# Ten bias additions on GpSimd moved from the aggregation into the first stage of a graph layer with a ternary feed-forward

## Chip, cores and metric

The kernel runs on one core of a Trainium2 chip. The metric is the time on the device in microseconds (us); the kernel before takes 337.06 us, the median of three runs from 336.26 to 338.64. All times of rows count from the start of the profiled span.

## What is computed

One graph layer over 1250 nodes of 512 features and 20000 edges sorted by destination, then a gated feed-forward with ternary weights. Cut to what matters:

```python
def gnn(x, src, dst, W_self, W_neigh, b):          # x: layer-normed nodes
    msg_sum = segment_sum(x[src], dst, 1250)
    neigh = msg_sum / maximum(deg, 1.0)[:, None]
    h = x @ W_self + neigh @ W_neigh + b
    h = where(h >= 0, h, 0.01 * h)
    return h / maximum(sqrt(sum(h * h, axis=1, keepdims=True)), 1e-12)

def quantize(w, group):                            # groups of 128 along a row
    scale = mean(abs(wg), axis=-1, keepdims=True) + 1e-5
    return clip(round(wg / scale), -1, 1) * scale

x = x + gnn(layernorm(x), src, dst, W_self, W_neigh, b)
g, u = ln(x) @ quantize(w_gate).T, ln(x) @ quantize(w_up).T
x = x + (silu(g) * u) @ quantize(w_down).T
```

The change touches only the place where `+ b` is computed.

## The kernel before

The 1250 nodes are ten tiles of 125 rows. Semaphores and the order of the code alone say what runs when: each engine's block is written out by hand, and an engine works strictly in that order. Three stages matter.

**First stage, 80 slots, eight to a tile (to about 107 us).** PE multiplies each layer-normed tile `xnT` with both weight halves in `w_sb` (L1374): slots 0 to 3 of a tile give `y` (neighbour part), slots 4 to 7 give the self part in bank 6, which ACT copies into `z[:, t, :]` (L847, semaphore `z_out`) in slot 2 of the next tile. ACT also writes the high part of `y` (L844); DVE computes the low part `y_lo` (L1122) from PSUM. Between the products PE builds the matrix of edge counts `a_t`, two chunks of 128 edges a slot (L1326, 157 chunks). For each chunk DVE makes a one-hot matrix `hot_dst` with a `tensor_scalar` over 16-bit numbers (L1138), and for each eight chunks `hot_src` with a `tensor_tensor` (L1129). Seven slots of `hot_dst` let DVE run ahead of PE. ACT and DVE move finished blocks from PSUM into `a_t` (L864, L1095). Layer norm of the next tiles (bn at L1025, xn at L1018) is DVE's too.

In the same slots 23 loads of feed-forward weights are made ternary, four blocks of 128 x 128 (jobs) a load: ACT takes magnitudes and their sums (L813, semaphore `abs_done`), GpSimd makes a load's thresholds in one small `tensor_scalar` (`scales_of(l)`, L693, `thr`), and DVE compares and multiplies, one `scalar_tensor_tensor` a job (L1039, "the ternary", reading `mag` and `raw` in SBUF). There are two magnitude buffers, so ACT's load l waits for the ternaries of load l - 2. For loads 0 to 3 GpSimd also runs a few checks (`check_windows`, L702 to L723).

**Between the stages (about 107 to 113 us)** four more loads are quantized (`mag_mid`, loads 23 to 26, `MID_LOADS` = 27). The other loads (`mag_late`) follow in the aggregation.

**Aggregation (about 108 to 158 us).** For each tile n, PE sums 10 x 2 products of `a_t` with `y` (L1418). Then DVE adds the sum to `z` (L1175, `neighbour_sum`, waits for `z_done`), takes the leaky part (L1181), and, when ACT has the norm, adds to `x_sb` (L1202, the residual), with bn_stats (L1208), and `shift` (L1217). ACT normalizes (`xn`, L877), and PE transposes that tile (L1315) in the middle of its sum four tiles on, so PE waits there if `xn` is late.

The bias stands in `bias_b`, 125 x 512 for a tile. GpSimd adds it to `z` in place (L735, `add_bias(t)`, 125 x 512 floats, both inputs in SBUF) and signals `z_done`. Before the change this comes when all thresholds up to load 26 are made and the matrix is joined: two tiles, then one after the thresholds of each aggregation step, the last five in a row. After it GpSimd scales the sums (`nscale`, L745) and has nothing to do until the feed-forward, which starts near 165 us and is bound by PE (L1481).

Of the kernel before, what the change touches and what calls it, by code (L numbers as in the profile page):

```python
# [31 lines left out]
ALU = mybir.AluOpType  # L32
# [11 lines left out]
def gnn_ffn(nc, x, src, dst, w_self, w_neigh, bias, w_gate, w_up, w_down, out):  # L44
# [3 lines left out]
    TP = 125  # L48
    NT = N // TP
# [6 lines left out]
    NB = 1 + NC // SC  # L56
# [45 lines left out]
    def place(name, shape, dt, region, offset=0):  # L102
        return nc.alloc_sbuf_tensor_at(name, shape, dt, offset=at[region] + offset)

    def small(name, shape, dt):
        width = {F32: 4, F32R: 4, I32: 4, BF16: 2, U16: 2}[dt]
        for n in shape[1:]:
            width *= n
        o = used["small"]
        used["small"] = o + -(-width // 32) * 32  # L110
        assert used["small"] <= 13184, 0
        return place(name, shape, dt, "small", o)
# [5 lines left out]
    z = place("z", [TP, NT, D], F32, "xz", GAP)  # L118
# [72 lines left out]
    bias_b = small("bias_b", [P, D], F32)  # L191
# [22 lines left out]
    with ExitStack() as ctx:  # L214
# [5 lines left out]
        def sem(name):  # L220
            return ctx.enter_context(nc.semaphore(name))
# [7 lines left out]
        bias_in = sem("bias_in")  # L229
# [15 lines left out]
        z_out = sem("z_out")  # L245
        z_done = sem("z_done")
# [8 lines left out]
        joined = sem("joined")  # L255
# [40 lines left out]
        for o, f in down_loads:  # L296
            n = min(4, NF - f)
            loads.append((w_down[o * P:(o + 1) * P, f * P:(f + n) * P], n))
            down_order += [(o, f + i) for i in range(n)]
        assert (2 * NF + 4) * P * 2 >= SBS * SB * P * 2  # L300
        job_load = [(l, i) for l, (_, n) in enumerate(loads) for i in range(n)]
        JOBS = len(job_load)
        load_end = [sum(n for _, n in loads[:l + 1]) for l in range(len(loads))]
        assert JOBS == 3 * NF * KD

# [58 lines left out]
        def down_loads_in(n):  # L364

            lo, hi = (MID_LOADS + max(0, min(NL, 2 * i)) for i in (n, n + 1))
            return range(lo, hi)
# [213 lines left out]
        def _(sp):  # L581
# [46 lines left out]
            for i, (_, f, down) in enumerate(by_dma):  # L628
                if i < TURN_SLOTS:
                    sp.wait_ge(ternary, load_end[len(loads) - RAWS + i])  # L630
                else:
                    sp.wait_ge(t_done, turn_T[by_dma[i - TURN_SLOTS]] + 1)
                for a in range(1 if down else 2):
                    for k in range(KD):
                        block = tq_d[:, k, f * P:(f + 1) * P] if down else tq_gu[:, a * NF + f, k * P:(k + 1) * P]
                        sp.dma_start(turned[:, turn_slot(i), a * D + k * P:a * D + (k + 1) * P], block,
                                     transpose=True).then_inc(t_turned[i % TURN_SLOTS], 16)
# [12 lines left out]
        def _(pool):  # L650
# [38 lines left out]
            def scales_of(l):  # L689

                js = slice(load_end[l] - loads[l][1], load_end[l])
                pool.wait_ge(abs_done, load_end[l])
                nc.gpsimd.tensor_scalar(thr[:, js], absum[:, js], 0.5 / P, 0.5 * Q_EPS, ALU.mult, ALU.add).then_inc(scales, 1)  # L693

            def check_windows(part):
# [22 lines left out]
                if part == 3:  # L718
# [3 lines left out]
                    pool.wait_ge(compared, 11)  # L722
                    nc.gpsimd.tensor_scalar(gap_ok[:], gap[:], 0.0, None, ALU.is_ge).then_inc(compared, 2)  # L723

            for l in range(MID_LOADS):
                scales_of(l)
                if l < 4:
                    check_windows(l)
            pool.wait_ge(bias_in, 16)
            pool.wait_ge(joined, NB - 1)  # L730

            def add_bias(t):

                pool.wait_ge(z_out, t + 1)
                nc.gpsimd.tensor_tensor(z[:, t, :], z[:, t, :], bias_b[0:TP, :], ALU.add).then_inc(z_done, 1)  # L735

            for t in range(2):
                add_bias(t)
            for n in range(NT):
                for l in down_loads_in(n):  # L740
                    scales_of(l)
                if n + 2 < NT:
                    add_bias(n + 2)

            nc.gpsimd.tensor_scalar(nscale[:], absum[:], 1.0 / P, Q_EPS, ALU.mult, ALU.add).then_inc(nscales, 1)  # L745

# [760 lines left out]
```

## Time and profile before

| | us |
|---|---|
| median of three runs | 337.06 |
| lowest, highest | 336.26, 338.64 |
| the profiled execution | 337.36 |
| its span | 335.6 |
| PE busy in the span | 315.7 (94%) |
| DVE busy | 305.3 (91%) |
| ACT busy | 236.9 (71%) |
| GpSimd (POOL) busy | 169.5 (51%) |

The span is the part of the profiled execution in which the program's instructions run; 1.8 us lie around it. PE's granted clock is 0.997 of full speed over the span. PE's matmuls are pipelined, and a matmul's end is modelled, so neighbouring rows overlap; the start of a matmul is the surer number. The same goes for instructions of DVE and ACT that stand close behind each other: they overlap by some tens of nanoseconds.

### The profile page before, as it was taken

The page shows a single profiled execution, that of the slowest core. Times are in us where ns is not written, and L with a number is a line of the kernel's source. Part 1 is how long each engine was busy: PE and PEld are TensorE (multiplying, and loading weights), DVE is VectorE, ACT ScalarE, POOL GpSimd, SP SyncE. Part 2 cuts the span into 40 slices and gives each one's busy share as a digit, 9 for nine tenths or more (in the row PEclk, how much of TensorE's full clock was granted, in tenths as well). Part 3 has the DMA queues.
Part 4 walks back from the last instruction along what each step waited for, and adds up shares of the span by engine and source line. Part 5 has one row for each costly group of instructions (what it writes and reads, how often), then busy time and mean ns, then how long its engine had stood idle before and what let it go on. Part 6 is the DMA issues. An engine that isn't in the chain of part 4 may idle for free.

```text
span 335.6 us, 5723 instructions
## 1 busy us (share of the span) xinstructions
PE 315.7 (94%) x1521; PEld 237.5 (71%) x1521; DVE 305.3 (91%) x782; ACT 236.9 (71%) x636; POOL 169.5 (51%) x235
## 2 busy tenths in 40 slices
PE   7989999999999999789989999999999999999991
PEld 3434454444554787577858898998989988899981
DVE  3599999998996899997999999999999999999993
ACT  2178988689885666354897677867868688676760
POOL 6015100010100445600016686989889897899992
PEclk9999999999999999999999999999999999999998
DMA  7992322223330321100001111111110100000305
GB/s 216 288 225 69 94 57 71 65 63 94 98 87 27 103 82 48 27 14 0 1 17 25 24 28 26 27 25 28 25 25 21 22 2 1 2 1 1 114 11 183
DMA packets 23610, 19.62 MB, mean 58 GB/s; under 512 B 15230, under 2 KB 16084, under 8 KB 23576
## 3 DMA queue, kind: packets, MB, share of 16 engines
q1 hardware_dynamic: 23498, 19.16, 21.3%
q8 instruction: 13, 0.21, 0.3%
q14 instruction: 21, 0.17, 0.2%
q10 hardware_dynamic: 78, 0.08, 0.1%
HBM read 13.73 MB, written 2.56 MB: 49 GB/s over the span
## 4 chain that ended last, share of the span: by engine, by line
PE 58%; DVE 27%; issue 4%; ACT 3%; DMA 3%; POOL 2%; SPq 1%; DVEq 0%; ACTq 0%; POOLq 0%
PE bank L1481 43%; PE bank L1374 7%; DVE hot_dst L1138 5%; DVE tq_gu L1039 4%; DVE tq_d L1039 4%; PE bank L1418 4%; DMA x_sb<-in_x 3%; PE bank L1326 2%; DVE hot_src L1129 2%; DVE bn L1025 1%; DVE z L1175 1%; DVE z L1181 1%; DVE x_sb L1202 1%; PE bank L1315 1%; DVE bn L1208 1%
## 5 line engine op out<-in xcount | busy, mean ns | idle before, releaser
L1481 PE MATMUL bank<-x_hi,t_gu 128*128 128x376 f32 (+1 forms) x264 | 94.5, 358 | 1.6 <-DVE g_acc L1270 0.7
L1481 PE MATMUL bank<-x_lo,t_gu 128*128 128x376 f32 (+1 forms) x264 | 92.8, 351 | 0.0
L1374 PE MATMUL bank<-w_sb,xnT 128*125 128x512 f32 x160 | 82.9, 606 | 1.7 <-DMA w_sb<-in_L_gnn_W_neigh 1.3
L1270 DVE SCALAR_TENSOR_TENSOR g_acc<-bank,nscale,g_acc 128x376 f32<-128x376 f32 (+1 forms) x99 | 63.8, 644 | 3.7 <-PE bank L1481 3.3
L1270 DVE SCALAR_TENSOR_TENSOR u_acc<-bank,nscale,u_acc 128x376 f32<-128x376 f32 (+1 forms) x99 | 63.6, 643 | 0.0
L754 POOL TENSOR_TENSOR acc<-acc,d_one 128x376 f32<-128x376 f32 (+1 forms) x58 | 63.3, 1094 | 0.0
L764 POOL TENSOR_TENSOR hh<-sg,u_acc 128x376 f32<-128x376 f32 (+1 forms) x32 | 35.1, 1096 | 50.6 <-ACT sg L974 50.6
L693 POOL TENSOR_SCALAR thr<-absum 128x4 f32<-128x4 f32 (+1 forms) x34 | 9.7, 285 | 99.8 <-ACT mag_early L813 75.5
L1481 PEld LDWEIGHTS bank<-x_hi,t_gu 128*128 128x128 f32 x264 | 49.6, 188 | 7.9 <-DVE g_acc L1270 1.8
L1481 PEld LDWEIGHTS bank<-x_lo,t_gu 128*128 128x128 f32 x264 | 49.6, 188 | 3.3
L1326 PEld LDWEIGHTS bank<-hot_dst,hot_src 128*126 128x126 bf16 x157 | 20.6, 135 | 41.4 <-DVE hot_dst L1138 26.3
L1481 PE MATMUL bank<-h_hi,t_d 128*128 128x376 f32 (+1 forms) x132 | 47.6, 361 | 0.2
L1481 PE MATMUL bank<-h_lo,t_d 128*128 128x376 f32 (+1 forms) x132 | 46.6, 353 | 0.0
L1418 PE MATMUL bank<-y_hi,a_t 125*125 125x512 f32 x100 | 40.2, 402 | 0.8 <-DVE a_t L1095 0.8
L1270 DVE SCALAR_TENSOR_TENSOR acc<-bank,nscale,acc 128x376 f32<-128x376 f32 (+1 forms) x62 | 39.3, 643 | 0.6 <-POOL acc L754 0.6
L1418 PE MATMUL bank<-y_lo,a_t 125*125 125x512 f32 x100 | 39.4, 394 | 0.0
L773 POOL TENSOR_TENSOR h_lo<-hh,h_hi 128x376 fp32r<-128x376 f32 (+1 forms) x32 | 35.0, 1094 | 4.9 <-ACT h_hi L921 4.9
L911 ACT ACTIVATE d_one<-bank,nscale 128x376 f32<-128x376 f32 (+1 forms) x58 | 34.8, 604 | 1.7 <-PE bank L1481 1.7
L1138 DVE TENSOR_SCALAR hot_dst<-iota_w,key 128x140 bf16<-128x140 uint16 (+4 forms) x150 | 34.4, 270 | 0.9 <-PE bank L1326 0.8
L813 ACT ACTIVATE mag_early<-raw 128x128 f32<-128x128 f32 x92 | 27.5, 304 | 7.7 <-DVE tq_gu L1039 6.5
L911 ACT ACTIVATE g_acc<-bank,nscale 128x376 f32<-128x376 f32 (+1 forms) x33 | 20.1, 608 | 17.3 <-PE bank L1481 16.5
L1039 DVE SCALAR_TENSOR_TENSOR tq_gu<-mag_early,thr,raw 128x128 bf16<-128x128 f32 x88 | 28.8, 354 | 2.8 <-POOL thr L693 2.7
(143 smaller groups left out, 550.5 us busy)
## 6 DMA issues: line engine op xcount, KB each, us to landing
raw<-in_L_ffn_w_gate SPq DMA_DIRECT2D x11, 256.0 KB, 2.7
raw<-in_L_ffn_w_up SPq DMA_DIRECT2D x11, 256.0 KB, 2.6
out_x<-x_sb SPq DMA_DIRECT2D x10, 224.0 KB
raw<-in_L_ffn_w_down SPq DMA_DIRECT2D x8, 256.0 KB, 2.7
turned<-tq_gu SPq DMA_TRANSPOSE x80, 2.4
w_sb<-in_L_gnn_W_neigh SPq DMA_DIRECT2D x1, 1024.0 KB, 7.2
w_sb<-in_L_gnn_W_self SPq DMA_DIRECT2D x1, 1024.0 KB, 8.4
x_sb<-in_x SPq DMA_DIRECT2D x2, 448.0 KB
```

The source lines that it names most:

```text
L754: nc.gpsimd.tensor_tensor(to, to, d_one[:, o, slot, 0:width(u)], ALU.add).then_inc(d_added, 1)
L764: nc.gpsimd.tensor_tensor(hh[:, u % 2, 0:w], sg[:, u % 2, 0:w], u_acc[:, u % 2, 0:w], ALU.mult).then_inc(h_done, 1)
L773: nc.gpsimd.tensor_tensor(h_lo[:, u % h_slots, 0:w], hh[:, u % 2, 0:w], h_hi[:, u % h_slots, 0:w].bitcast(F32), ALU.subtract).then_inc(hlo ...
L813: nc.scalar.activation(mag_of(j), raw_of(j), ACT.Abs, accum_out=absum[:, j:j + 1]).then_inc(abs_done, 1)
L911: nc.scalar.activation(to, bank_of(u, what)[:, 0:width(u)], ACT.Copy, scale=nscale[:, j:j + 1]).then_inc(act_took, 1)
L1039: nc.vector.scalar_tensor_tensor(out=tq_of(j), in0=mag_of(j), scalar=thr[:, j:j + 1], in1=raw_of(j), op0=ALU.is_gt, op1=ALU.mult).then_inc ...
L1138: nc.vector.tensor_scalar(to, numbers, key[:, c:c + 1], None, ALU.is_equal).then_inc(hot_made, 1)
L1270: nc.vector.scalar_tensor_tensor(out=to, in0=bank_of(u, what)[:, 0:w], scalar=nscale[:, j:j + 1], in1=to, op0=ALU.mult, op1=ALU.add).then_ ...
L1326: nc.tensor.matmul(bank[k % 3][0:TQ, 0:NT * WIN].rearrange("p (s d) -> p s d", d=WIN)[:, :, lo:hi], hot_src[:, c // SB % SBS, c % SB, 0:TQ ...
L1374: last = nc.tensor.matmul(to[0:TP, :], xnT[:, t, k * TP:(k + 1) * TP], w_sb[:, k, half * D:(half + 1) * D], start=k == 0, stop=k == KD - 1)
L1418: last = nc.tensor.matmul(bank[4 + n % 2][0:TP, :], a_t[0:TP, s, n * TP:(n + 1) * TP], y[:, s, :], start=s == 0 and y is y_hi, stop=s == N ...
L1481: last = nc.tensor.matmul(bank_of(u, what)[:, 0:width(u)], w, parts[h], start=h == 0, stop=h == 1)
```

## The change

The ten additions leave their place behind the thresholds of load 26. They now stand in the loop over loads 0 to 26 itself: behind the threshold of load `BIAS_AT[t]` comes the addition for tile t, which still waits for ACT's copy of that tile (`z_out`). The first waits for the load of the bias. The wait for the joined matrix is gone. The instructions themselves are the same; no other engine's code is touched.

```diff
+            BIAS_AT = [4, 5, 7, 10, 12, 15, 17, 20, 22, 23]
             for l in range(MID_LOADS):
                 scales_of(l)
                 if l < 4:
                     check_windows(l)
-            pool.wait_ge(bias_in, 16)
-            pool.wait_ge(joined, NB - 1)
-
-            def add_bias(t):
-
-                pool.wait_ge(z_out, t + 1)
-                nc.gpsimd.tensor_tensor(z[:, t, :], z[:, t, :], bias_b[0:TP, :], ALU.add).then_inc(z_done, 1)
-
-            for t in range(2):
-                add_bias(t)
+                if l in BIAS_AT:
+                    t = BIAS_AT.index(l)
+                    if t == 0:
+                        pool.wait_ge(bias_in, 16)
+                    pool.wait_ge(z_out, t + 1)
+                    nc.gpsimd.tensor_tensor(z[:, t, :], z[:, t, :], bias_b[0:TP, :], ALU.add).then_inc(z_done, 1)
             for n in range(NT):
                 for l in down_loads_in(n):
                     scales_of(l)
-                if n + 2 < NT:
-                    add_bias(n + 2)
```

On GpSimd (POOL), in the first stage, these rows stand behind the last window check (`gap_ok`) in the kernel before. `thr` rows are thresholds of a load each, `z` rows are additions; the first 19 thresholds belong to the first stage, the next four to loads 23 to 26, the rest to the aggregation.

```order
L723 TENSOR_SCALAR gap_ok<-gap 128x31
L693 TENSOR_SCALAR thr<-absum 128x4 x19
L693 TENSOR_SCALAR thr<-absum 128x3
L693 TENSOR_SCALAR thr<-absum 128x4 x2
L693 TENSOR_SCALAR thr<-absum 128x3
L735 TENSOR_TENSOR z<-z,bias_b 125x512 x2
L693 TENSOR_SCALAR thr<-absum 128x4 x2
L735 TENSOR_TENSOR z<-z,bias_b 125x512
L693 TENSOR_SCALAR thr<-absum 128x4
L693 TENSOR_SCALAR thr<-absum 128x3
```

In the changed kernel, from the same `gap_ok` row on:

```order
L723 TENSOR_SCALAR gap_ok<-gap 128x31
L693 TENSOR_SCALAR thr<-absum 128x4
L735 TENSOR_TENSOR z<-z,bias_b 125x512
L693 TENSOR_SCALAR thr<-absum 128x4
L735 TENSOR_TENSOR z<-z,bias_b 125x512
L693 TENSOR_SCALAR thr<-absum 128x4 x2
L735 TENSOR_TENSOR z<-z,bias_b 125x512
L693 TENSOR_SCALAR thr<-absum 128x4 x3
L735 TENSOR_TENSOR z<-z,bias_b 125x512
L693 TENSOR_SCALAR thr<-absum 128x4 x2
L735 TENSOR_TENSOR z<-z,bias_b 125x512
```

The run of 19 thresholds (loads 4 to 22) is cut up: additions of tiles 0 to 4 stand behind the thresholds of loads 4, 5, 7, 10 and 12. Further on, those of tiles 8 and 9 stand around the threshold of load 23, the 128x3 row, and no addition stands in the aggregation.

```order
L693 TENSOR_SCALAR thr<-absum 128x4 x2
L735 TENSOR_TENSOR z<-z,bias_b 125x512
L693 TENSOR_SCALAR thr<-absum 128x3
L735 TENSOR_TENSOR z<-z,bias_b 125x512
L693 TENSOR_SCALAR thr<-absum 128x4 x2
L693 TENSOR_SCALAR thr<-absum 128x3
L693 TENSOR_SCALAR thr<-absum 128x4 x3
L693 TENSOR_SCALAR thr<-absum 128x3
L693 TENSOR_SCALAR thr<-absum 128x4 x2
```

Here the additions of tiles 8 and 9 are the two `z` rows, and everything behind them is a threshold.

## Rows read from the trace of the kernel before

**Rows 1.** Busy time of each engine in stretches; their columns stand in the first line.

```profile
core 0: us, PE busy (x) PEld busy (x) DVE busy (x) ACT busy (x) POOL busy (x), PEclk, DMA share, GB/s
35.00:60.00 25.00, 24.66 (x103) 12.91 (x103) 23.83 (x103) 22.05 (x78) 1.94 (x7) 1.00 0.23 66
...
96.00:107.00 11.00, 11.00 (x43) 5.49 (x42) 8.41 (x37) 6.62 (x17) 0.19 (x1) 1.00 0.20 59
130.00:145.00 15.00, 11.74 (x56) 9.09 (x57) 14.62 (x36) 6.08 (x20) 7.68 (x7) 1.00 0.12 25
145.00:160.00 15.00, 15.00 (x79) 12.00 (x77) 12.62 (x32) 7.45 (x19) 0.00 (x0) 1.00 0.02 4
```

**Rows 2.** The chain of waits by line: 36 to 41 us, 41 to 84, 84 to 107.

```profile
by line: issue 27.3%; ACT mag_early L813 17.3%; ACT a_t L864 11.7%; ACT xnT L850 11.6%; PE bank L1315 8.6%; PE bank L1374 8.6%; DVE tq_gu L1039 5.0%; PE bank L1326 4.4%; POOL thr L693 4.0%; ACT y_hi L844 1.4%; ACT hot_src L796 0.9%; ACTq L8
by line: DVE hot_dst L1138 26.6%; DVE tq_gu L1039 24.3%; DVE hot_src L1129 9.8%; issue 8.4%; ACT mag_early L813 5.9%; DVE bn L1025 5.7%; DVE y_lo L1122 5.5%; DVE xn L1018 4.8%; DVE a_t L1095 2.7%; ACT a_t L864 2.2%; POOL thr L693 0.9%; DVE 
by line: PE bank L1374 77.1%; PE bank L1326 17.6%; PE bank L1315 3.7%; PE bank L552 3.2%; issue 0.2%
```

**Rows 3.** Waits of PE, 107 to 145 us: total, times, longest, in us.

```profile
PE bank L1315 <- ACT xn L877: 3.7, 3, 1.9
```

**Rows 4.** GpSimd's additions in order of time: start, us, engine, line, operation, count.

```profile
113.11 2.59 POOL L735 TENSOR_TENSOR z<-z,bias_b 125x512 f32<-125x512 f32 x2
...
122.28 1.67 POOL L735 TENSOR_TENSOR z<-z,bias_b 125x512 f32<-125x512 f32 x1
...
131.79 7.18 POOL L735 TENSOR_TENSOR z<-z,bias_b 125x512 f32<-125x512 f32 x5
```

**Rows 5.** DVE in the aggregation: three instructions, then groups (busy us, mean ns, idle before).

```profile
113.07 1.48 DVE L1039 SCALAR_TENSOR_TENSOR tq_d<-mag_mid,thr,raw 128x128 bf16<-128x128 f32 x1
...
131.72 0.75 DVE L1175 SCALAR_TENSOR_TENSOR z<-bank,rdeg,z 125x512 f32<-125x512 f32 x1
...
133.55 1.78 DVE L1202 SCALAR_TENSOR_TENSOR x_sb<-z,inv,x_sb 125x512 f32<-125x512 f32 x1
...
L1039 DVE SCALAR_TENSOR_TENSOR tq_d<-mag_late,thr,raw 128x128 bf16<-128x128 f32 x26 | 9.9, 445 | 0.0
L1202 DVE SCALAR_TENSOR_TENSOR x_sb<-z,inv,x_sb 125x512 f32<-125x512 f32 x10 | 8.5, 850 | 0.1
L1175 DVE SCALAR_TENSOR_TENSOR z<-bank,rdeg,z 125x512 f32<-125x512 f32 x10 | 7.4, 744 | 1.9 <-PE bank L1418 1.9
...
L1039 DVE SCALAR_TENSOR_TENSOR tq_d<-mag_mid,thr,raw 128x128 bf16<-128x128 f32 x14 | 6.2, 503 | 0.8 <-POOL thr L693 0.7
```

**Rows 6.** DVE's three costliest groups, 36 to 84 us.

```profile
L1138 DVE TENSOR_SCALAR hot_dst<-iota_w,key 128x140 bf16<-128x140 uint16 (+4 forms) x83 | 18.9, 268 | 0.0
L1039 DVE SCALAR_TENSOR_TENSOR tq_gu<-mag_early,thr,raw 128x128 bf16<-128x128 f32 x53 | 17.3, 348 | 1.9 <-POOL thr L693 1.9
L1129 DVE TENSOR_TENSOR hot_src<-iota,hot_src 128x1000 bf16<-128x1000 uint16 x11 | 7.5, 681 | 0.0
```

**Rows 7.** A window check of GpSimd and DVE's hot_dst beside it.

```profile
22.78 0.64 POOL L702 TENSOR_TENSOR win_lo<-rel,win_lo 128x157 f32<-128x157 f32 x1
22.95 0.52 DVE L1138 TENSOR_SCALAR hot_dst<-iota_w,key 128x140 bf16<-128x140 uint16 x1
```

**Rows 8.** Thresholds (41 to 84 us as group), copies of z, hot_dst and its use, DVE's waits.

```profile
L693 POOL TENSOR_SCALAR thr<-absum 128x4 f32<-128x4 f32 x12 | 3.8, 313 | 38.1 <-ACT mag_early L813 38.1
40.55 0.19 POOL L693 TENSOR_SCALAR thr<-absum 128x4 f32<-128x4 f32 x1 [3.83 <-ACT mag_early L813]
...
108.97 0.20 POOL L693 TENSOR_SCALAR thr<-absum 128x3 f32<-128x3 f32 x1 [11.29 <-ACT mag_mid L813]
92.94 0.58 ACT L847 ACTIVATE z<-bank 125x512 f32<-125x512 f32 x1
101.29 0.59 ACT L847 ACTIVATE z<-bank 125x512 f32<-125x512 f32 x1
102.14 0.64 DVE L1138 TENSOR_SCALAR hot_dst<-iota_w,key 128x200 bf16<-128x200 uint16 x3
102.99 0.30 PE L1326 MATMUL bank<-hot_dst,hot_src 128*126 128x140 bf16 x2
DVE tq_gu L1039 <- POOL thr L693: 2.7, 4, 0.8
```

## The prediction

> **What bounds the kernel now.** I began with the table of busy time by stretch [rows 1]. From 35 to 60 us PE and DVE are both near full, 24.66 and 23.83 of 25 us. From 96 to 107 us PE is full and DVE has 8.41 of 11. From 130 to 145, in the aggregation, PE is busy for only 11.74 of 15 us while DVE has 14.62; behind 145 PE has 15.00 of 15. For the first stage the table does not say which of the two sets the pace; the chain of waits does [rows 2]. From 36 to 41 us it passes through ACT and PE and hardly touches DVE (tq_gu 5.0% alone). From 41 to 84 us it lies on DVE: hot_dst 26.6, tq_gu 24.3, hot_src 9.8, bn 5.7, y_lo 5.5, xn 4.8%, together 76.7%. From 84 to 107 us it lies on PE alone.
>
> In the aggregation the view of waits shows what DVE's lateness costs PE: its transposes wait for ACT's xn three times, 3.7 us in total, the longest 1.9 [rows 3]. ACT makes xn from DVE's residual and shift, so DVE stands behind those waits.
>
> Now the ten additions [rows 4]: two at 113.11 us take 2.59, so 1.3 us each, and five in a row 7.18. The one at 122.28 takes 1.67, so it was itself held up by 0.4. Beside them some of DVE's instructions are long [rows 5]: a ternary at 113.07 us takes 1.48, where the mean of the first stage is 0.35 [rows 6], and ends at 114.55, where the first addition does (114.4). A residual at 133.55 takes 1.78. The sum z<-bank,rdeg,z at 131.72, whose first input lies in PSUM, runs beside an addition in 0.75, its usual time (the ten of them mean 744 ns). So an addition holds one DVE instruction that reads SBUF as ternaries do, up to its own end: 1.1 us.
>
> **What the change takes away.** All ten additions leave the stretch from 113 to 139 us. What they cost DVE there follows from the means [rows 5]: 14 ternaries of mag_mid at 503 instead of 348 ns are 2.2 us, 26 of mag_late at 445 are 2.5, ten residuals at 850 instead of some 744 (a sum of the same shape) are 1.1. Together 5.8 us, and with a shift and a leak some 6.2. PE cannot take back more than it waited, 3.7 us [rows 3], because behind 145 us it is full. As DVE gets 6 us and needs 3.7, I take all of the 3.7. The lower end is 1.5, if DVE's freed time comes too late for the first two waits.
>
> The wait for the last join goes too; GpSimd had nothing else to do there. The threshold for load 26, which stood behind two additions, comes some 2 us earlier, but DVE takes it only behind the first leak. Nothing.
>
> **What it puts in.** Each addition stands behind one threshold and in front of the next. From 41 to 84 us GpSimd is idle 38.1 us before 12 thresholds [rows 8], 3.2 us each, against 1.3 for an addition: the next threshold, and the ternaries that wait for it, are not late. Tiles 7 and 8 are not copied yet at their place: ACT writes them at 92.94 and 101.29 us [rows 8], 0.6 us each, so GpSimd waits for it and adds from 93.6 and 101.9. Nothing is due before either ends. Tile 9 stands behind the threshold at 108.97 us, where DVE waits for each threshold: I count one stalled ternary, 1.1 us, and up to 0.4 for the next threshold. That is less than the 2.2 us which tiles 0 and 1 cost there before, so it costs the end nothing and eats part of DVE's 6.
>
> For the other nine the question is what DVE does beside them. From 36 to 84 us [rows 6] hot_dst has 18.9 us, the ternaries 17.3, hot_src 7.5. Ternaries and hot_src read two tensors of SBUF. That hot_dst, with one, is held too, the window checks early in the program show [rows 7]: beside GpSimd's 0.64 us at 22.78 a hot_dst takes 0.52 us where the mean is 0.27, and both end within 0.05 us of each other. What looks free (y_lo, a_t with PSUM; bn) is 5.5 + 2.7 + 5.7 = 13.9% of the chain [rows 2], a sixth of DVE's part. So some four in five additions meet an exposed instruction at once.
>
> The Trainium skill draws the same line between instructions: GPSIMD Engine Reference, section 8 (Key points), has GpSimd contend with VectorE instructions that run in a two-port mode or have two SBUF inputs, and VectorE: DVE Perf Modes, section on the perf-mode tier table, puts a 16-bit tensor_scalar from SBUF into the fastest of these modes. It speaks against this change: by that rule hot_dst stalls with each addition, and the first stage costs more than the aggregation gives back. The 0.52 us agrees. Were only two-input instructions held, the cost would go towards the low end below.
>
> One stall: 1.1 us where the next instruction is exposed, about 0.6 where a free one comes first; 0.8 x 1.1 + 0.2 x 0.6 = 1.0 us. Tile 1 stands behind the threshold at 40.55 us [rows 8], and tiles 1 to 6 all start between there and 84 us, where the chain is on DVE: 6 x 1.0 = 6.0. DVE's four waits for thresholds (2.7 us, the longest 0.8 [rows 8]) may swallow 0.4 of it. Tile 0, near 37 us, falls where the chain is not on DVE, and DVE then waits 0.7 us for that threshold anyway: of 1.1 I leave 0.4. Tile 7 falls where the chain is on PE and DVE has a wait of 0.7 ahead: nothing. Tile 8, at 101.9: of the three hot_dst from 102.14 us (0.64 together), the first is used by PE at 102.99 [rows 8], some 0.6 to 0.9 us later, so 1.1 leaves 0.3. Sum: 6.0 - 0.4 + 0.4 + 0.3 = 6.3 us. Bounds: from below six stalls of 0.5, 3.0 us (a stall like the old average, under rival 1); from above nine of 1.13 (1.48 - 0.35), 10.2. I take 6.3, since the ternaries that were met stand at 1.0 to 1.1.
>
> **The sum.** +6.3 - 3.7 = +2.6 us. The profiled execution took 337.36 us (span 335.6), so 340.0. It lies 0.3 above the median of the three runs, 337.06; against that median the forecast is 339.7 us, 0.8% more. Everything behind 145 us is only moved.
>
> **Rivals.**
> 1. Not slower: the stalls of the first stage are cheap. The ten old additions took 6.2 us from DVE, 0.6 each, because some met bn_stats or a PSUM input. At 0.5 us for tiles 1 to 6 and nothing for the others the cost is 3.0 and the change -0.7: 336.4 us. The point from which it decides is a cost of 3.7, about 0.6 for each of the six. Against it: free instructions are a sixth of DVE's part of the chain [rows 2], fewer than in the aggregation. Chance 25%.
> 2. Nothing swallows anything: nine additions delay PE by 1.1 each, because PE and DVE take turns in being late and the first stalls use up the leads. 9.9 - 3.7 = +6.2: 343.3 us. For it: both are at 95% or more [rows 1]. Against it: DVE has 2.6 us of 11 to spare behind 96 us. Chance 10%.
> 3. The aggregation gives back only 1.5 us, since tile 9's addition now delays the quantizing at 109 us, on which DVE's first sum hangs. 6.3 - 1.5 = +4.8: 341.9 us. Against it: DVE still comes out 5 us ahead of before. Chance 10%.
>
> **How the numbers follow.** My forecast has 55%, with a range of its own from 338.3 to 341.3 us. A measurement of this kernel can tell about 1% (3.4 us) from no change, so the bounds are 333.7 and 340.4. Slower by more: a third of the forecast's share (0.19), rival 2 and most of rival 3 (0.18), together 0.37. Faster by over 1% needs nearly the whole 3.7 us and no cost at all: 0.03. The rest, 0.60, lies within 1%. The range from 335.8 to 342.8 takes in rival 1, rival 3 and the forecast and leaves out most of rival 2.
>
> **What would show it.** In the changed kernel's profile: nine additions of z before the aggregation and a tenth right behind the first mag_mid threshold; beside six to eight of them a hot_dst, hot_src or ternary of 1.2 to 1.5 us; that threshold, at 108.97 us now, some 6 us later; no long residual or leak in the aggregation, and PE's waits for xn gone. The forecast is wrong if hot_dst beside an addition keeps its 0.27 us, if that threshold moves by less than 4 us, or if PE still waits for xn by more than 1 us.

## The result, and the profile after

The changed kernel takes 339.93 us (median of 8 runs, 338.86 to 340.56) against 337.32 us before (8 runs): a ratio of 1.0082, 95% interval 1.0056 to 1.0108, so 1.9 to 3.6 us slower. The forecast was 339.7 us and 2.6 us. The sum came out; its terms did not quite, as the stages show.

The profiled execution has a span of 338.1 us. Two rows of PE's timeline in each kernel mark the stages: the first use of `hot_dst` and the first product with `a_t`. In the kernel before (columns: start, duration):

```profile
18.38 0.64 PE L1326 MATMUL bank<-hot_dst,hot_src 128*126 128x140 bf16 x3 [1.03 <-DVE hot_dst L1138]
...
108.25 0.50 PE L1418 MATMUL bank<-y_hi,a_t 125*125 125x512 f32 x1 [0.76 <-DVE a_t L1095]
...
163.63 0.42 PE L1481 MATMUL bank<-x_hi,t_gu 128*128 128x376 f32 x1
```

In the changed kernel:

```profile
16.79 0.64 PE L1321 MATMUL bank<-hot_dst,hot_src 128*126 128x140 bf16 x3
...
114.19 0.49 PE L1413 MATMUL bank<-y_hi,a_t 125*125 125x512 f32 x1 [0.76 <-DVE a_t L1090]
...
165.26 0.42 PE L1476 MATMUL bank<-x_hi,t_gu 128*128 128x376 f32 x1
```

Line numbers behind the change are 5 lower. The differences: the first stage goes from 89.9 to 97.4 us (+7.5), the aggregation from 55.4 to 51.1 (-4.3). The start is 1.6 us earlier, because the first loads of x and the edges landed earlier in this execution (DVE waits 0.2 us for x there, 1.3 in the profile before): over the twelve profiles of this study it lies between 16.8 and 19.2 us whatever the kernel. The feed-forward took 0.9 us more, of which below. So +7.5 - 4.3 = +3.2 us by stages, inside the interval of the times.

GpSimd's additions in the changed kernel (of tiles 1, 3, 4, 8 and 9, with the threshold of load 23 in front of the last), which answer to [rows 4]:

```profile
39.80 1.27 POOL L735 TENSOR_TENSOR z<-z,bias_b 125x512 f32<-125x512 f32 x1
...
60.48 1.53 POOL L735 TENSOR_TENSOR z<-z,bias_b 125x512 f32<-125x512 f32 x1
...
70.03 1.27 POOL L735 TENSOR_TENSOR z<-z,bias_b 125x512 f32<-125x512 f32 x1
...
107.39 1.26 POOL L735 TENSOR_TENSOR z<-z,bias_b 125x512 f32<-125x512 f32 x1 [4.14 <-ACT z L842]
...
114.92 0.20 POOL L693 TENSOR_SCALAR thr<-absum 128x3 f32<-128x3 f32 x1 [6.27 <-ACT mag_mid L808]
115.19 1.28 POOL L735 TENSOR_TENSOR z<-z,bias_b 125x512 f32<-125x512 f32 x1
```

And what DVE does beside tiles 1, 3, 4 and 8:

```profile
39.78 1.44 DVE L1034 SCALAR_TENSOR_TENSOR tq_gu<-mag_early,thr,raw 128x128 bf16<-128x128 f32 x1
...
60.71 1.38 DVE L1133 TENSOR_SCALAR hot_dst<-iota_w,key 128x220 bf16<-128x220 uint16 x1
...
70.06 1.29 DVE L1133 TENSOR_SCALAR hot_dst<-iota_w,key 128x140 bf16<-128x140 uint16 x1
...
107.35 1.36 DVE L1133 TENSOR_SCALAR hot_dst<-iota_w,key 128x140 bf16<-128x140 uint16 x1
```

Each of the nine additions in the first stage, and tile 9's too, met such an instruction at once: five ternaries and five `hot_dst`, 1.29 to 1.46 us where they have 0.35 and 0.27 alone. `hot_dst`, with one input, is held as firmly as the ternary. The `hot_dst` end 0.05 to 0.08 us behind their addition (71.35 against 71.30 for tile 4), the ternaries 0.15 (41.22 against 41.07 for tile 1), and the difference is that of their own lengths. So, as an estimate from these rows, the held instruction does its whole own work from some 0.2 us before the recorded end of the addition on. The next group answers to [rows 5]: DVE in the aggregation of the changed kernel.

```profile
L1197 DVE SCALAR_TENSOR_TENSOR x_sb<-z,inv,x_sb 125x512 f32<-125x512 f32 x10 | 7.5, 748 | 0.1
L1034 DVE SCALAR_TENSOR_TENSOR tq_d<-mag_late,thr,raw 128x128 bf16<-128x128 f32 x26 | 7.1, 344 | 0.0
```

The residual is back at 748 ns (850 before) and the ternaries at 344 (445 before). PE's waits from 107 to 165 us, answering to [rows 3], are two, and none is for xn:

```profile
PE bank L1413 <- DVE a_t L1090: 0.8, 1, 0.8
PE bank L1321 <- DVE hot_dst L1133: 0.2, 1, 0.2
```

### The profile page after: what moved, and what is told of

It is laid out like the page before. It is cut to its first block, busy times and chain, and to the rows that moved or that the text cites. A ratio compares the mean times of both kernels' runs of the same rounds, so it can differ in the third digit from the quotient of the medians.

```text
span 338.1 us, 5723 instructions
## 1 busy us (share of the span) xinstructions
PE 318.6 (94%) x1521; PEld 239.4 (71%) x1521; DVE 309.8 (92%) x782; ACT 237.2 (70%) x636; POOL 168.6 (50%) x235
## 4 chain that ended last, share of the span: by engine, by line
PE 68%; DVE 21%; issue 4%; ACT 2%; POOL 2%; DMA 1%; SPq 1%; DVEq 0%; ACTq 0%; POOLq 0%
PE bank L1476 42%; PE bank L1413 13%; PE bank L1369 8%; DVE hot_dst L1133 6%; DVE tq_gu L1034 6%; PE bank L1321 2%; DVE hot_src L1124 2%; PE bank L1310 2%; DMA e_i<-in_dst 1%; DVE y_lo L1117 1%; DVE bn L1020 1%; POOL acc L749 1%; ACT mag_early L808 1%; PE bank L1454 1%; DVE xn L1013 1%
## 5 line engine op out<-in xcount | busy, mean ns | idle before, releaser
L1476 PEld LDWEIGHTS bank<-x_hi,t_gu 128*128 128x128 f32 x264 | 50.3, 191 | 6.8 <-DVE g_acc L1265 1.0
L693 POOL TENSOR_SCALAR thr<-absum 128x4 f32<-128x4 f32 (+1 forms) x34 | 10.0, 294 | 90.4 <-ACT mag_early L808 67.2
L1133 DVE TENSOR_SCALAR hot_dst<-iota_w,key 128x140 bf16<-128x140 uint16 (+4 forms) x150 | 39.9, 306 | 0.9 <-PE bank L1321 0.8
L1321 PE MATMUL bank<-hot_dst,hot_src 128*126 128x140 bf16 (+6 forms) x157 | 28.9, 263 | 6.8 <-DVE hot_dst L1133 6.5
L1034 DVE SCALAR_TENSOR_TENSOR tq_gu<-mag_early,thr,raw 128x128 bf16<-128x128 f32 x88 | 32.9, 399 | 1.4 <-POOL thr L693 1.3
```

The costliest lines, as they stand in the source:

```text
L1034: nc.vector.scalar_tensor_tensor(out=tq_of(j), in0=mag_of(j), scalar=thr[:, j:j + 1], in1=raw_of(j), op0=ALU.is_gt, op1=ALU.mult).then_inc ...
L1133: nc.vector.tensor_scalar(to, numbers, key[:, c:c + 1], None, ALU.is_equal).then_inc(hot_made, 1)
L1321: nc.tensor.matmul(bank[k % 3][0:TQ, 0:NT * WIN].rearrange("p (s d) -> p s d", d=WIN)[:, :, lo:hi], hot_src[:, c // SB % SBS, c % SB, 0:TQ ...
L1476: last = nc.tensor.matmul(bank_of(u, what)[:, 0:width(u)], w, parts[h], start=h == 0, stop=h == 1)
```

## The experiments

The ten runs stand in one table of stages, each taken from the same rows of PE as above. The ratio is to the kernel before, run on the same chip beside it. The first stage's length can be off by 0.3 us, as a late start is partly made up within a few chunks; by this it reads 0.3 us too short in e6_twice and 0.2 in e8_gap. From PE's sixth chunk to its thirty-first, at some 36 us, all twelve profiles take the same time within 0.1 us.

| run | first stage, us | aggregation, us | ratio to before (95%) |
|---|---|---|---|
| before | 89.9 | 55.4 | 1 |
| changed | 97.4 | 51.1 | 1.0082 (1.0056 to 1.0108) |
| e9_changed, once more | 97.3 | 51.1 | 1.0081 (1.0058 to 1.0105) |
| e1_none | 89.9 | 51.1 | 0.9876 (0.9841 to 0.9911) |
| e2_narrow | 90.0 | 51.2 | 0.9872 (0.9836 to 0.9908) |
| e10_ends | 90.7 | 51.1 | 0.9885 (0.9849 to 0.9921) |
| e11_middle | 96.3 | 51.1 | 1.0040 (1.0012 to 1.0068) |
| e6_twice | 99.2 | 51.1 | 1.0139 (1.0114 to 1.0164) |
| e7_one_input | 92.6 | 51.1 | 0.9944 (0.9918 to 0.9970) |
| e4_gate | 89.9 | 53.2 | 0.9951 (0.9917 to 0.9985) |
| e5_gate_one | 90.4 | 52.1 | 0.9928 (0.9894 to 0.9961) |
| e8_gap | 89.7 | 51.1 | 0.9853 (0.9828 to 0.9879) |

**No additions.**

The kernel before, without the additions and their waits (in part):

```diff
-            def add_bias(t):
-
-                pool.wait_ge(z_out, t + 1)
-                nc.gpsimd.tensor_tensor(z[:, t, :], z[:, t, :], bias_b[0:TP, :], ALU.add).then_inc(z_done, 1)
...
-                dve.wait_ge(z_done, t + 1)
+                dve.wait_ge(z_out, t + 1)
```

> Leaves the bias out: GpSimd adds nothing, DVE's sum waits for ACT's copy of z instead. My theory (an addition holds one DVE instruction up to its own end): without any addition the first stage keeps its old length and the aggregation loses PE's waits for xn, 3.7 to 4.3 us, so 333.0 to 333.7 us against 337.3 before, and no ternary over 0.6 us. Rival (the additions cost nothing by themselves, it is where GpSimd's queue stands that counts): the same as this within 0.3%, so this run alone does not part them, the narrow one does.

Measured 332.66 us beside 336.57 for the kernel before, 0.3 under the forecast's lower end. The first stage has its old length to 0.1 us, the aggregation the changed kernel's. So the additions cost the kernel before 4.2 us (ratio) in the aggregation and nothing elsewhere, and moving them gives all of that back.

**The same places and waits, 8 columns wide.**

```diff
-                    nc.gpsimd.tensor_tensor(z[:, t, :], z[:, t, :], bias_b[0:TP, :], ALU.add).then_inc(z_done, 1)
+                    nc.gpsimd.tensor_tensor(z[:, t, 0:8], z[:, t, 0:8], bias_b[0:TP, 0:8], ALU.add).then_inc(z_done, 1)
```

> The changed kernel with the ten additions cut to 8 of 512 columns (the rest of the bias left out), all waits and places as changed. My theory: the stall is as long as GpSimd's instruction, so nearly all of the cost goes: 333.0 to 334.2 us, as without additions. Rival (thresholds late behind the additions' waits for z_out, or the order of the queue): still 339 to 340 us, since places and waits are the same.

Measured 332.71 us, the same as without additions (forecast from 333.0 up). GpSimd's timeline shows the addition of tile 4 in its place behind the threshold of load 12, at 0.20 us:

```profile
66.57 0.19 POOL L693 TENSOR_SCALAR thr<-absum 128x4 f32<-128x4 f32 x1 [4.24 <-ACT mag_early L808]
66.84 0.20 POOL L735 TENSOR_TENSOR z<-z,bias_b 125x8 f32<-125x8 f32 x1
```

The queue, the order and the waits for `z_out` are all there; with these short instructions they cost 0.3 us together by the stages (90.0 + 51.2 against 89.9 + 51.1, unrounded 141.22 against 140.95), and the times do not tell them from nothing. What costs is how long GpSimd's instruction runs. The rival is out.

**Which tiles carry the cost.** In e10_ends tiles 1 to 6 are narrow, in e11_middle the other four.

```diff
-                    nc.gpsimd.tensor_tensor(z[:, t, :], z[:, t, :], bias_b[0:TP, :], ALU.add).then_inc(z_done, 1)
+                    cols = 8 if 1 <= t <= 6 else D
+                    nc.gpsimd.tensor_tensor(z[:, t, 0:cols], z[:, t, 0:cols], bias_b[0:TP, 0:cols], ALU.add).then_inc(z_done, 1)
```

> The changed kernel with the additions of tiles 1 to 6 cut to 8 of 512 columns (their bias left out for the rest); tiles 0, 7, 8 and 9 are whole. They stand where the chain is not on DVE. My theory: 0.2 to 0.7 us for tile 0, nothing for 7 and 9, 0.5 for 8: 0.7 to 1.2 us over the kernel with ten narrow additions, so some 3.3 us under the kernel before. Rival (each addition in the first stage costs 1.1 us wherever it stands): 3.3 us over the narrow kernel.

> The reverse: tiles 1 to 6 whole, the additions of tiles 0, 7, 8 and 9 cut to 8 columns. My theory: these six carry nearly all of the cost, 6.0 to 6.8 us over the kernel with ten narrow additions, 2.0 to 2.6 us over the kernel before. Rival (equal cost of 0.75 us for each of the ten): 4.5 us over the narrow kernel, as before.

Over the narrow kernel the first stage grows by 0.7 us with tiles 0, 7 and 8 whole, and by 6.3 with tiles 1 to 6 whole. In times: 333.54 us (-3.9 by the ratio, forecast -3.3) and 338.54 (+1.3, forecast 2.0 to 2.6). The six stand where the chain is on DVE and cost 1.05 each; the others 0.25 each on average. Position decides, as the prediction's chain of waits said. For e11 the time is a little better than its stages (+6.3 - 4.3 = +2.0), within its interval of 0.4 to 2.3 us.

**Some additions twice.** Tiles 2, 3 and 5, one behind the other.

```diff
+                    if t in (2, 3, 5):
+                        nc.gpsimd.tensor_tensor(z[:, t, :], z[:, t, :], bias_b[0:TP, :], ALU.add).then_inc(once, 1)
+                        pool.wait_ge(once, (2, 3, 5).index(t) + 1)
                     nc.gpsimd.tensor_tensor(z[:, t, :], z[:, t, :], bias_b[0:TP, :], ALU.add).then_inc(z_done, 1)
```

> The changed kernel, with the additions of tiles 2, 3 and 5 made twice one behind the other (these tiles get the bias twice). All three stand where the chain of the first stage is on DVE. My theory: each further addition delays DVE and PE by 1.0 to 1.1 us, so the kernel takes 3.0 to 3.3 us more than the changed kernel. Rival (the first addition only uses up slack, or it is the wait for z_out that delays): less than 1 us more.

Measured 342.15 us, 1.9 us more than the changed kernel beside it (340.21); I had expected 3.0 to 3.3. PE's starts against those of the changed kernel show why: the second addition of tile 2 shifts them by 1.1 us, that of tile 5 by 1.0, that of tile 3 by only 0.2. That is 2.3 us; 0.2 of it is missing from the total because the one addition of tile 0 costs 0.2 less here than in the changed kernel, as it does in e10_ends. GpSimd's and DVE's timelines at tile 3:

```profile
62.77 1.53 POOL L737 TENSOR_TENSOR z<-z,bias_b 125x512 f32<-125x512 f32 x1
64.38 1.84 POOL L739 TENSOR_TENSOR z<-z,bias_b 125x512 f32<-125x512 f32 x1
```

```profile
64.49 0.60 DVE L1038 SCALAR_TENSOR_TENSOR tq_gu<-mag_early,thr,raw 128x128 bf16<-128x128 f32 x2
65.02 0.68 DVE L1024 BATCH_NORM_STATS2 bn<-x_sb 125x6 f32<-125x512 f32 x1
65.73 0.18 DVE L1027 BATCH_NORM_AGGREGATE mv<-bn 125x2 f32<-125x6 f32 x1
65.83 0.62 DVE L1137 TENSOR_SCALAR hot_dst<-iota_w,key 128x140 bf16<-128x140 uint16 x2
```

The second addition starts while DVE is at a `hot_dst` with two ternaries behind it, waits for them (1.84 us for 1.27), and then runs beside bn_stats, which keeps its 0.68. By the time a `hot_dst` comes the addition is nearly done. The miss is the forecast's "each", not the mechanism: a row shows the stall being dodged.

**One input instead of two.**

```diff
-                    nc.gpsimd.tensor_tensor(z[:, t, :], z[:, t, :], bias_b[0:TP, :], ALU.add).then_inc(z_done, 1)
+                    nc.gpsimd.tensor_scalar(z[:, t, :], z[:, t, :], 0.0, None, ALU.add).then_inc(z_done, 1)
```

> The changed kernel with each addition replaced by a tensor_scalar of GpSimd on the same 125x512 floats (adds 0.0, one input; the bias is left out). It tells whether GpSimd's second input is what holds DVE. If any GpSimd instruction on SBUF holds DVE to its end: long ternaries and hot_dst beside each, and the kernel changes only with GpSimd's own duration. If only two-input instructions of GpSimd do: no DVE instruction over 0.6 us beside them and 332.7 to 333.5 us, as without additions. The window checks of before (tensor_scalar at 27.1 to 27.7 us, a hot_dst beside it 0.1 us longer) speak for the first.

Measured 335.39 us, and neither answer is right. The first stage is 92.6 us: 2.7 over that without additions, where the two-input form costs 7.5. GpSimd's instruction takes longer, and DVE's beside it are held for only part of it (GpSimd's row, then DVE's):

```profile
68.79 1.49 POOL L735 TENSOR_SCALAR z<-z 125x512 f32<-125x512 f32 x1
```

```profile
68.83 0.62 DVE L1133 TENSOR_SCALAR hot_dst<-iota_w,key 128x140 bf16<-128x140 uint16 x1
69.37 0.68 DVE L1124 TENSOR_TENSOR hot_src<-iota,hot_src 128x1000 bf16<-128x1000 uint16 x1
69.97 0.44 DVE L1133 TENSOR_SCALAR hot_dst<-iota_w,key 128x180 bf16<-128x180 uint16 x2
```

A `hot_dst` of 0.62 us, then a whole `hot_src` at its usual 0.68 while GpSimd's instruction still runs. The `hot_dst` ends at 69.45 us; less its 0.27 alone it was let go at 69.18 by this estimate, 0.4 us behind the start of GpSimd's instruction, and by the same sum a two-input addition lets DVE go only after 1.05 us (71.35 less 0.27 against 70.03). The edit changes the operation together with the number of inputs, so the runs do not show which of the two matters, and how the hardware divides the access stays open; nothing further was run on it.

**Additions in the aggregation, behind residuals.** The kernel before with one more wait from tile 3 on:

```diff
                 if n + 2 < NT:
+                    if n >= 1:
+                        pool.wait_ge(x1_done, n)
                     add_bias(n + 2)
```

> The kernel before, but from the fourth tile on each addition in the aggregation also waits for the end of a residual (x1_done), behind which DVE does bn_stats, an instruction with one input of SBUF that was not lengthened. My theory: the five additions that ran in a row no longer meet ternaries and residuals, PE's second and third wait for xn (1.9 and 1.1 us) go, the first (0.6) stays: -3.0 us, 334.3 us (333.5 to 335.0). Rival (bn_stats is held as well, or DVE's lateness there has another cause): 337 us as before, with PE's waits for xn kept.

Measured 335.12 us (0.9951: -1.7 us, forecast -3.0). The aggregation shrinks by 2.2 us. PE's third wait for xn is gone; the first stays, and of the second, 1.9 us before, 0.7 is left:

```profile
PE bank L1317 <- ACT xn L879: 1.4, 2, 0.7
```

DVE's timeline at tile 5, whose addition starts at 134.47 and ends at 135.76:

```profile
134.42 0.69 DVE L1210 BATCH_NORM_STATS2 bn<-x_sb 125x6 f32<-125x512 f32 x1
135.15 0.18 DVE L1212 BATCH_NORM_AGGREGATE mv<-bn 125x2 f32<-125x6 f32 x1
135.25 0.13 DVE L1217 RECIPROCAL rs<-sd 125x1 f32<-125x1 f32 x1
135.41 0.37 DVE L1219 SCALAR_TENSOR_TENSOR shift<-mv,rs 125x1 f32<-125x1 f32 x1
```

Three instructions pass untouched and only `shift` is held, 0.37 for 0.16. The place is as cheap as expected; the size of the gain was not, since some 3.5 us of DVE's old stalls (tiles 0 to 2 and the ternary beside tile 3) are still there and keep a part of the second wait as well.

**The same with tile 0 in the first stage, behind load 20.**

```diff
...
+                if l == 20:
+                    pool.wait_ge(bias_in, 16)
+                    pool.wait_ge(z_out, 1)
+                    nc.gpsimd.tensor_tensor(z[:, 0, :], z[:, 0, :], bias_b[0:TP, :], ALU.add).then_inc(z_done, 1)
...
-            for t in range(2):
-                add_bias(t)
+            add_bias(1)
```

> As the gated kernel, and the addition of tile 0 alone stands in the first stage behind the threshold of load 20, where the chain is on PE. My theory: its stall there is hidden in DVE's lead, DVE is 1.1 us earlier in the aggregation, so PE's first wait for xn (0.6) goes too: 333.3 us (332.8 to 334.2), the same as without any addition. Rival (each addition in the first stage costs 1.1 us wherever it stands): 1.1 minus 0.6 above the gated kernel, 334.8 us.

Measured 334.22 us, between the two. The ternary beside it is held (1.37 us), and of that 0.5 reaches PE: DVE's lead there is some 0.6 us, not 1.1. The aggregation is 1.0 shorter than in the gated kernel: PE's first wait is gone as forecast, but the second still has 0.7 us, which the forecast left out here as it did for the gated kernel.

**Additions in DVE's own wait.** The version that these runs point to:

```diff
+                if l == LOADS1 - 1:
+                    pool.wait_ge(bias_in, 16)
+                    pool.wait_ge(hot_made, NC)
+                    for t in range(3):
+                        add_bias(t)
...
-                if n + 2 < NT:
+                if 1 <= n < NT - 2:
+                    pool.wait_ge(x1_done, n)
                     add_bias(n + 2)
```

> Additions of tiles 0 to 2 behind the last hot_dst (hot_made at its last count), where DVE waits for PE's last chunks from 104 to 109 us; tiles 3 to 9 in the aggregation, each behind a residual as in the gated kernel. My theory: nothing is stalled by the first three, the others only hold shift and one ternary by 0.2 to 0.3 us, so all of PE's waits for xn go: 0 to 0.5 us above the kernel without additions, some 3.5 us under the kernel before (1.0%). Rival (an addition always takes its 1.1 us from DVE and DVE has no slack): no faster than the gated kernel, 1.5 us under before.

Measured 332.52 us beside 336.99 for before: 0.9853 (0.9828 to 0.9879), 5.0 us faster by the ratio (forecast some 3.5), and as fast as the kernel that adds nothing. GpSimd's three additions, then DVE in the same stretch:

```profile
104.68 3.72 POOL L728 TENSOR_TENSOR z<-z,bias_b 125x512 f32<-125x512 f32 x3 [7.02 <-issue]
```

```profile
104.30 0.24 DVE L1139 TENSOR_SCALAR hot_dst<-iota,key 128x50 bf16<-128x50 uint16 x1 [0.32 <-PE bank L1327]
106.18 0.18 DVE L1096 TENSOR_TENSOR a_t<-bank,a_t 126x10 f32 x1 [1.64 <-ACT a_t L865]
107.59 0.60 DVE L1096 TENSOR_TENSOR a_t<-bank,a_t 126x420 fp32r<-126x420 f32 x1 [1.23 <-PE bank L1327]
```

The three fit into two waits of DVE, 1.64 and 1.23 us, and beside joins that read PSUM; waits and joins are as long in e1_none, without any addition. So these three hold nothing. The other seven hold a `shift` or a ternary by 0.2 to 0.3 us each, and PE has no wait for xn left.

**The changed kernel again.**

> The changed kernel itself once more, beside the others on one chip: 2.6 us over the kernel before (2.0 to 3.4), the first stage 7 to 7.5 us longer and the aggregation some 4.3 us shorter in its profile, whatever the landing of the first loads does.

Measured 340.21 us beside 336.99, stages as in the first profile: +7.4 and -4.3.

## Why the prediction was right, and where its terms were off

- **Mechanism.** An addition holds one DVE instruction, two-input or 16-bit one-input alike, nearly to the addition's own end (to some 0.2 us before it): shown by the rows after and by the narrow kernel, in which only the length of GpSimd's instruction changed. An instruction that DVE has already begun is not held; the addition waits for it (that of tile 3, at 60.48 us, behind an `xn` begun at 60.26, takes 1.53 us for 1.27).
- **What the change takes away: 3.7 us, measured 4.3.** The step "PE cannot take back more than it waited" used the idle time in the view of waits. Counted from the first product with `a_t`, the three transpositions started at 21.95, 29.17 and 35.60 us and now start at 21.15, 26.22 and 31.30. That is 0.8, another 2.2 and another 1.3 us earlier, where the waits were 0.63, 1.93 and 1.13: each wait cost about 0.2 us more than its idle time. That all of it comes back, with DVE no longer late, was right; rival 3 (1.5 us) is out, as the aggregation is 51.1 us in every version in which DVE is early enough.
- **Tiles 1 to 6: 6.0 - 0.4, measured 6.3.** Two terms were too kind. I had one addition in five meet a free instruction first; all six met an exposed one. And the 0.4 us that DVE's waits for thresholds were to swallow was not swallowed: those waits hang on ACT, which hangs on DVE, and they moved along. In the changed kernel the ternary at 80.84 us still waits 0.84 us for its threshold before the addition holds it. DVE's waits for thresholds do fall from four (2.7 us) to two (1.3), but the two that are gone are those at tiles 0 and 7, outside this stretch.
- **Tiles 0, 7 and 8: 0.7, measured 0.7** (e10_ends), tile 7 costing nothing.
- **The rest.** 6.3 and 0.7 make 7.0 over the narrow kernel; the whole changed kernel has 7.4, and 7.3 in its second profile. Most of the difference lies at tile 0. PE waits there for a `hot_dst`, first in the changed kernel, then in e10_ends:

```profile
36.84 0.29 PE L1321 MATMUL bank<-hot_dst,hot_src 128*126 128x180 bf16 x1 [0.49 <-DVE hot_dst L1133]
```

```profile
37.31 0.29 PE L1322 MATMUL bank<-hot_dst,hot_src 128*126 128x180 bf16 x1 [0.26 <-DVE hot_dst L1134]
```

Tile 0 costs 0.7 us in both profiles of the changed kernel and 0.5 in e10_ends; in the changed kernel GpSimd starts that addition 0.2 us later against PE. What remains, 0.1 us or so, is as much as the two profiles of the changed kernel differ by: tile 8 costs 0.5 in one of them and 0.4 in the other.

- **The sum.** 6.3 - 3.7 = 2.6 was forecast, 7.5 - 4.3 = 3.2 stands in the stages, 2.8 in the ratio. Both terms were about a sixth too small, by 1.2 and 0.6 us, and the errors cancelled in part. That the total came within 0.6 us by the stages and 0.2 by the ratio is in this part luck; that the cost outweighs the gain is not. Rival 1 (3.0 us of cost) and rival 2 (9.9) are out by the first stage's length, though it lies between the forecast and rival 2.
- **Threshold of load 23.** At 114.92 us it came 5.9 us later (forecast some 6), with a start 1.6 us earlier.

## What to carry to other kernels

Work on GpSimd is not free because GpSimd is idle: a two-input instruction of 1.27 us took 1.1 us from DVE wherever DVE's next instruction read SBUF with two inputs or in 16 bits. Place it by what DVE does: in DVE's own waits for PE, beside PSUM reads or bn_stats, and never in a stretch whose chain lies on DVE. In the aggregation the ten took some 6.2 us from DVE, of which 4.3 reached PE; in the first stage nine took 9.6 (an estimate: the ten held lengths but tile 9's, less 0.27 or 0.35 each), of which 7.5 did. The same ten instructions in the gaps cost nothing that the times show.

## What the runs showed that I had not expected

A one-input GpSimd instruction on the same 125x512 floats is slower than the two-input one (1.49 us against 1.27, both beside DVE) and yet costs DVE much less, 0.3 us each in the first stage.

The feed-forward's beginning has its own clock noise. Here are busy time and granted clock in two profiles whose feed-forward starts at nearly the same time: e1_none from 167.8 to 171.2 us, then e8_gap for the stretch ahead of that and for the same stretch:

```profile
167.80:171.20 3.40, 3.40 (x19) 2.46 (x17) 3.37 (x8) 2.88 (x7) 0.99 (x1) 1.00 0.13 29
```

```profile
159.00:167.80 8.80, 6.68 (x38) 5.41 (x36) 8.59 (x20) 8.15 (x16) 0.00 (x0) 1.00 0.02 5
167.80:171.20 3.40, 3.40 (x13) 3.40 (x14) 3.37 (x8) 1.59 (x4) 0.98 (x1) 0.50 0.12 27
```

PE's clock is at its upper level (2.4 GHz) throughout in the one and at its lower level of 1.2 GHz for 3.4 us in the other, where PE starts 13 matmuls in place of 19. Ahead of it PE was busy for 6.68 of 8.80 us at the upper level, and e1_none shows nearly the same (6.70); so the rows do not say what sets the drop off. The first profile of the changed kernel and that of e2_narrow have such a drop too, with a mean clock of 0.85 and 0.82 from 168 to 176 us. With the drop the part behind the aggregation is 172.9 us long (changed kernel, e8_gap) or 172.5 (e2_narrow), in the nine other profiles it is 171.9 to 172.1, and the second profile of the changed kernel is among these. So it belongs to the execution and not to the change, and it makes a single profile misleading by up to 0.9 us.
